# Two projections of four dropped for late batches, and VectorE's products with the sines written to the other 64 partitions

## The chip, the cores and the metric

One core of one Trainium2 chip runs the whole program. The metric is the device time of one execution in microseconds; the time before is the median of 3 runs, 332.85 us. Times of a timeline are counted from the start of the profiled execution's span.

## The reference

Two layers on x of shape (8, 256, 128): a batch b is x[b], 256 tokens of 128 features. The change touches only the first attention's q and k:

```python
def heads(W):
    return (x @ W.T).reshape(B, S, H, hd).transpose(0, 2, 1, 3)   # 16 heads of 8 features
Q = _rope(heads(Wq))
K = _rope(heads(Wk))
V = heads(Wv)
# _rope(t): t1, t2 = halves of the 8 features; [t1*cos - t2*sin, t2*cos + t1*sin]
s = (q @ k + LAMBDA * (q*q) @ (k*k)) * inv_sqrt_d, causal, softmax, times v
# once with Q, K and once with both halves rotated; outputs combined, times Wo
x = x + attention0(layernorm(x))
x = x + ffn0(layernorm(x))            # 128 -> 512 relu -> 128
x = x + attention1(layernorm(x))      # 16 heads, not causal
x = x + ffn1(layernorm(x))            # 384 wide, silu(gate) * up
```

## The kernel before

Each engine has its own program, written out by hand over *phases* and *slots*. A phase is one layer's attention of one batch (16 phases, layer 0's batches 0 to 7 first); a phase has 16 slots. In slot s of phase i TensorE computes the scores of head-slot s of phase i+1 (L901 and L902 in layer 0), whose row maxima VectorE takes (`maximum`, L734 and L736), and the shifted scores of phase i (L928, L930), whose exponential ScalarE takes (L572). In layer 0 POOL sets the future to zero in every odd slot (`cut`: L452 and then L455, "masking" in the text), and TensorE multiplies four heads of probabilities at a time by v (`pv`, L954). The maxima are transposed on TensorE twice per phase (`max_rows`, L911 and L912), copied by ScalarE (L576) and put into a row of the stack QS by DMA. Everything else (FFN, norms, output projections) is placed in slots by the tables STEP and STAGE_A. Engines take their instructions strictly in order and wait on semaphores. Slots are counted through from phase 0: slot 16 is slot 0 of phase 1; slots -16 to -1 lie ahead of phase 0.

PSUM has 8 banks. Three hold scores, two shifted scores, one the outputs; banks 6 and 7 are shared by all the other work, in an order that `bank_uses` works out: `into(name)` makes TensorE wait until the bank's last user has emptied it.

The stage of layer 0 for one batch (STAGE_A for batches 3 to 7, the late ones; batches 0 to 2 are done ahead of all phases):

- `variance` on VectorE (L667, L671), then `norm` on POOL (L413 to L423), transposes on TensorE (`norm_t0`, L851), copy to XT by ScalarE (L529);
- `project` on TensorE (L865): q by wq and, into the other half of the same bank, its *rotated twin* by wrq, whose columns are those of wq with the halves of each head exchanged; the same for k in another bank. Each of these float32 products of 128x128 by 128x256 shows as two records. Then v (L871) into bank 6;
- `product` on VectorE (L693): TQ = bank (128x512) times TAB (cosines, then sines with the sign of the rotation in them), once for q and once for k;
- `rotate` on POOL (L432): QR = left half + right half of TQ, once for q and once for k;
- `square` (L534) and a 16-bit copy (`high`, L546) on ScalarE, the remainder (`low`, L698) on VectorE, and DMAs through a scratch in HBM into the stacks QS and KS for the batch's phase.

In partition order the features are laid out so that partitions 0 to 63 hold the first halves of all heads and 64 to 127 the second halves: row j*16 + slot is feature j of the head of that slot.

## Time and profile before

| | |
|---|---|
| median of 3 runs | 332.85 us (332.72 to 333.4) |
| the profiled execution | 332.69 us, its span 330.9 us |
| TensorE matmul busy | 296.2 us (90%) |
| TensorE weight load busy | 212.9 us (64%) |
| VectorE busy | 252.3 us (76%) |
| ScalarE busy | 217.7 us (66%) |
| POOL busy | 160.7 us (49%) |
| mean granted TensorE clock | 0.973 |

A timeline row has start, duration (of several merged instructions, from the first start to the last end), engine, line, operation, tiles out<-in, shape, count, and in brackets the idle time before it and what ended it. A granted clock of 1.00 is 2.4 GHz, of 0.50 it is 1.2 GHz. The span's layer-0 stage for late batches lies between 22 and 105 us.

### The profile page before, as it was taken

To read this page: it belongs to the slowest core of one execution; us is meant where nothing else is said; L and a number is where in the kernel's file an instruction comes from. 1 tells how busy PE (TensorE), PEld (TensorE's weight loads), DVE (VectorE), ACT (ScalarE), POOL (GpSimd) and SP (SyncE) were. 2 spreads that over 40 slices of the span, in tenths; PEclk is the share of its full clock that TensorE was granted. 3 is DMA by queue.
4 is the path that set the end of the run, shared out by engine and by line. 5 is a ranking of instruction groups with operands and counts; after the bars stand their busy time and mean duration, and the time that the engine had idled before them with its cause. 6 is when DMAs were issued, how large, how long until landed. Compare 5 with 4: busy or idle time off the path is not lost.

```text
span 330.9 us, 8407 instructions
## 1 busy us (share of the span) xinstructions
PE 296.2 (90%) x2852; PEld 212.9 (64%) x2852; DVE 252.3 (76%) x999; ACT 217.7 (66%) x494; POOL 160.7 (49%) x376
## 2 busy tenths in 40 slices
PE   7648779698999899999999999999999999998945
PEld 4526556476677677767776676766767676665634
DVE  7878869688778767677768677679797979795564
ACT  8652575557568858586767768597777767677621
POOL 5641674866775867767677614523241404040210
PEclk9986799899999999999999999999999999999997
DMA  7976214311313113121211110020212010100001
GB/s 198 317 167 154 64 53 111 113 31 36 99 48 115 49 52 80 51 81 38 70 25 54 32 57 26 24 58 27 72 27 75 24 43 26 42 2 18 15 3 32
DMA packets 23178, 21.59 MB, mean 65 GB/s; under 512 B 2944, under 2 KB 20096, under 8 KB 23136
## 3 DMA queue, kind: packets, MB, share of 16 engines
q1 hardware_dynamic: 23136, 21.05, 22.9%
q8 instruction: 23, 0.38, 0.5%
q14 instruction: 19, 0.16, 0.2%
HBM read 13.18 MB, written 7.34 MB: 62 GB/s over the span
## 4 chain that ended last, share of the span: by engine, by line
PE 64%; DVE 12%; POOL 10%; issue 7%; ACT 6%; POOLq 0%; ACTq 0%; DVEq 0%
PE bank L954 15%; PE bank L928 7%; PE bank L984 5%; PE bank L997 5%; PE bank L904 4%; PE bank L905 4%; PE bank L932 4%; PE bank L1029 3%; POOL XN L423 3%; PE bank L1037 3%; PE bank L851 2%; ACT PB L572 2%; PE bank L902 2%; POOL RS L416 2%; DVE JUNK L736 2%
## 5 line engine op out<-in xcount | busy, mean ns | idle before, releaser
L572 ACT ACTIVATE PB<-bank 128x384 f32<-128x384 f32 (+1 forms) x256 | 134.6, 544 | 57.0 <-PE bank L930 34.1
L739 DVE TENSOR_REDUCE NM<-bank 128x2 f32<-128x512 f32 x128 | 83.8, 684 | 25.0 <-PE bank L905 24.8
L928 PE MATMUL bank<-QS,KS 128*128 128x256 f16 x256 | 70.5, 276 | 2.6 <-ACT PB L572 1.9
L954 PE MATMUL bank<-PB,VP 128*32 128x256 f32 (+1 forms) x1024 | 62.1, 360 | 2.5 <-POOL PB L455 1.7
L734 DVE CUSTOM_DVE_ANT_0 JUNK<-bank,MSF 128x128 bf16<-128x128 f32 x128 | 36.5, 285 | 26.1 <-PE bank L902 25.9
L736 DVE CUSTOM_DVE_ANT_0 JUNK<-bank,MSF 128x256 bf16<-128x256 f32 x128 | 53.7, 420 | 0.0
L954 PEld LDWEIGHTS bank<-PB,VP 128*32 128x32 f32 x1024 | 26.8, 109 | 25.6 <-issue 10.3
L455 POOL TENSOR_SCALAR_AFFINE_SELECT PB<-PB 128x512 f32<-128x512 f32 x64 | 41.0, 641 | 0.0
L902 PE MATMUL bank<-KS,QS 96*128 96x256 f16 x128 | 36.1, 285 | 0.0
L904 PE MATMUL bank<-KS,QS 96*128 96x256 f16 x128 | 35.2, 275 | 0.0
L905 PE MATMUL bank<-KS,QS 96*128 96x256 f16 x128 | 34.7, 271 | 0.0
L932 PE MATMUL bank<-QS,KS 128*128 128x256 f16 x128 | 34.4, 271 | 0.0
L901 PE MATMUL bank<-KS,QS 96*128 96x128 f16 x128 | 29.2, 230 | 5.7 <-DMA KS<-scr 3.5
L928 PEld LDWEIGHTS bank<-QS,KS 128*128 128x128 f16 x256 | 24.8, 97 | 12.2 <-ACT PB L572 9.6
L452 POOL TENSOR_TENSOR HELD<-EPSC 128x1 f32<-128x1 f32 x64 | 13.7, 213 | 38.1 <-ACT PB L572 38.0
L413 POOL TENSOR_TENSOR VE<-MV,EPSC 128x2 f32<-128x2 f32 x32 | 6.7, 208 | 49.0 <-DVE MV L671 49.0
L478 POOL TENSOR_TENSOR xs<-xs,Y 128x256 f32<-128x256 f32 x6 | 4.3, 725 | 49.3 <-DVE Y L748 49.3
L930 PE MATMUL bank<-QS,KS 128*128 128x128 f16 x128 | 28.1, 220 | 0.0
L423 POOL TENSOR_SCALAR XN<-xs,NMN,RS 128x128 f32<-128x128 f32 x54 | 25.4, 479 | 2.8
L416 POOL TENSOR_TENSOR RS<-VE,EPSC 128x2 f32<-128x2 f32 x32 | 22.4, 700 | 2.5
L851 PE MATMUL bank<-IDF,XN 128*128 128x128 f32 x64 | 13.5, 294 | 9.8 <-POOL XN L423 4.2
L901 PEld LDWEIGHTS bank<-KS,QS 96*128 96x128 f16 x128 | 12.8, 100 | 13.5 <-DVE NM L736 6.2
(95 smaller groups left out, 601.0 us busy)
## 6 DMA issues: line engine op xcount, KB each, us to landing
scr<-PR SPq DMA_DIRECT2D x16, 256.0 KB, 2.9
QS<-scr SPq DMA_DIRECT2D x16, 128.0 KB, 2.7
QS<-scr SPq DMA_DIRECT2D x32, 64.0 KB, 2.9
KS<-scr SPq DMA_DIRECT2D x32, 64.0 KB, 2.8
KS<-scr SPq DMA_DIRECT2D x16, 128.0 KB, 3.1
scr<-PR SPq DMA_DIRECT2D x16, 128.0 KB, 1.9
out_x<-xs SPq DMA_DIRECT2D x8, 128.0 KB, 1.9
W<-in_w SPq DMA_DIRECT2D x1, 576.0 KB, 5.9
```

The lines of the kernel that those rows point to most:

```text
L455: pool.affine_select(out=pr, in_=pr, compare_op=ALU.is_ge, fill=0.0, base=0, pattern=[[0, 4], [1, P]], channel_multiplier=-1).then_inc(s_c ...
L572: act.activation(PB[:, s % RING, 0:n], scored(i, s)[:, 0:n], ACT.Exp).then_inc(s_e, 1)
L734: dve.tensor_tensor_reduce(JUNK[:, g % 3, 0], o[:, 0:P], MSF[:, 1], -1.0, 3e38, ALU.add, ALU.min, accum_out=m[:, s, 0:1])
L736: dve.tensor_tensor_reduce(JUNK[:, g % 3, 1:3], o[:, P:3 * P].rearrange("q (n k) -> q n k", n=2), MSF[:, :], -1.0, 3e38, ALU.add, ALU.min, ...
L739: dve.tensor_reduce(m[:, s, 0:2], o[:, :].rearrange("q (n k) -> q n k", n=2), AX.X, ALU.max, negate=True).then_inc(s_mx, 1)
L901: pe.matmul(o[:, 0:P], q[:, 0:P], k[:, 0:P], start=True, stop=True)
L902: ins = pe.matmul(o[:, P:3 * P], q[:, P:2 * P], k[:, :], start=True, stop=True)
L904: pe.matmul(o[:, 0:S], q[:, 0:P], k[:, :], start=True, stop=True)
L905: ins = pe.matmul(o[:, S:2 * S], q[:, P:2 * P], k[:, :], start=True, stop=True)
L928: pe.matmul(o[:, 0:S], k[:, 0:P], q[:, :], start=True, stop=True)
L932: ins = pe.matmul(o[:, S:2 * S], k[:, P:2 * P], q[:, :], start=True, stop=True)
L954: ins = pe.matmul(o, v, pr, start=(g % 2 == 0 and kt == 0), stop=True, skip_group_check=True)
```

## The change

For batches 3 to 7 the rotated twins are not projected. `project_late` puts q (256 columns) and k (256 columns) into the two halves of one bank, bank 7, always; `product_both` replaces the two products: part 0 multiplies both by the cosines (128 partitions, 512 elements each), part 1 multiplies by the sines in two instructions over 64 partitions, each reading one half of the partitions and writing the other half. Part 0 runs in k's slot, part 1 one slot later, and only the end of part 1 frees the bank. The sines' signs now come from the half that is read, so `rotate_both` on POOL subtracts, q and k in one instruction of 128x512. It takes the place of the two rotations at the slot behind (`rot`), and the squares' slots move: sq_q by one slot (batch 3 from -4 to -3, 4 from 8 to 9, 5 from 19 to 20, 6 from 31 to 32, 7 from 47 to 48); batch 7's k rotation moves from slot 52 to slot 47. Batches 0 to 2 are as they were.

```diff
@@ -68,12 +68,12 @@
 LAST_T = (3, 4, 0, 1)
 
 
-STAGE_A = {3: dict(bn=None, norm=None, xT=-8, q=-6, k=-5, v=-3, rot_q=-4, rot_k=-3, sq_q=-4, sq_k=-2, hi=-1, lo=1),
-           4: dict(bn=-2, norm=0, xT=3, q=5, k=6, v=7, rot_q=7, rot_k=8, sq_q=8, sq_k=10, hi=12, lo=14),
-           5: dict(bn=6, norm=10, xT=13, q=15, k=17, v=18, rot_q=18, rot_k=20, sq_q=19, sq_k=21, hi=22, lo=24),
-           6: dict(bn=18, norm=22, xT=27, q=28, k=29, v=30, rot_q=30, rot_k=32, sq_q=31, sq_k=33, hi=35, lo=37),
-           7: dict(bn=34, norm=39, xT=43, q=44, k=45, v=46, rot_q=46, rot_k=52, sq_q=47, sq_k=53, hi=55, lo=57)}
-A_BANK = {3: (6, 6, 7, 6), 4: (6, 6, 7, 6), 5: (6, 7, 6, 7), 6: (6, 6, 7, 6), 7: (6, 6, 7, 6)}
+STAGE_A = {3: dict(bn=None, norm=None, xT=-8, q=-6, k=-5, v=-3, rot=-3, sq_q=-3, sq_k=-2, hi=-1, lo=1),
+           4: dict(bn=-2, norm=0, xT=3, q=5, k=6, v=7, rot=8, sq_q=9, sq_k=10, hi=12, lo=14),
+           5: dict(bn=6, norm=10, xT=13, q=15, k=17, v=18, rot=19, sq_q=20, sq_k=21, hi=22, lo=24),
+           6: dict(bn=18, norm=22, xT=27, q=28, k=29, v=30, rot=31, sq_q=32, sq_k=33, hi=35, lo=37),
+           7: dict(bn=34, norm=39, xT=43, q=44, k=45, v=46, rot=47, sq_q=48, sq_k=53, hi=55, lo=57)}
+A_BANK = {3: (6, 7, 6), 4: (6, 7, 6), 5: (6, 7, 6), 6: (6, 7, 6), 7: (6, 7, 6)}
 
 
 LOADS = {(L, b): (L * B + b - 2, "mid") for L in range(2) for b in range(B) if (L, b) > (0, 1)}
@@ -123,7 +123,7 @@
         uses += [(-100 + 4 * b + n, k, (name, b)) for n, (name, k) in
                  enumerate((("xT0", p), ("q", 2 + 3 * p), ("k", 3 + 3 * p), ("v0", 4 + 3 * p)))]
     for b, a in STAGE_A.items():
-        uses += [(a[step], k, (name, b)) for name, step, k in zip(("xT0", "q", "k", "v0"), ("xT", "q", "k", "v"), A_BANK[b])]
+        uses += [(a[step], k, (name, b)) for name, step, k in zip(("xT0", "qk0", "v0"), ("xT", "q", "v"), A_BANK[b])]
     for i in range(NPH):
         uses += [(H * (i - 1) + m0_slot(i - 1), 6 if phase(i - 3)[0] == 1 else 7, ("mr0", i)), (H * i + m1_slot(i), 6, ("mr1", i))]
         L, b = ORDER[i]
@@ -431,6 +431,12 @@
                 p = b % 2
                 pool.tensor_tensor(QR[p][:, n, 0], TQ[p][:, n, 0:S], TQ[p][:, n, S:2 * S], ALU.add).then_inc(s_rot, 1)
 
+            def rotate_both(b):
+                pool.wait_ge(*emptied("qk0", b))
+                pool.wait_ge(s_lo, 2 * b - 2)
+                p = b % 2
+                pool.tensor_tensor(QR[p][:, :, 0], TQ[p][:, :, 0:S], TQ[p][:, :, S:2 * S], ALU.subtract).then_inc(s_rot, 2)
+
             def spread_v(i):
                 L, b = ORDER[i]
                 if L == 0:
@@ -499,9 +505,8 @@
                     for b, a in STAGE_A.items():
                         if a["norm"] == H * i + s:
                             norm(0, b)
-                        for n, step in enumerate(("rot_q", "rot_k")):
-                            if a[step] == H * i + s:
-                                rotate(b, n)
+                        if a["rot"] == H * i + s:
+                            rotate_both(b)
                     if i == -1 and s == 3:
                         pool.wait_ge(s_vz, 2)
                         for p in range(2):
@@ -692,6 +697,17 @@
                 dve.wait_ge(*filled(name, b))
                 dve.tensor_tensor(TQ[p][:, n], psum(name, b)[:, :], TAB[:, n], ALU.mult).then_inc(*empties(name, b))
 
+            def product_both(b, part):
+                p, half = b % 2, P // 2
+                qk = psum("qk0", b)[:, :].rearrange("q (n t) -> q n t", n=2)
+                if part == 0:
+                    dve.wait_ge(*filled("qk0", b))
+                    dve.tensor_tensor(TQ[p][:, :, 0:S], qk, TAB[:, :, 0:S], ALU.mult)
+                    return
+                dve.tensor_tensor(TQ[p][0:half, :, S:2 * S], qk[half:P], TAB[half:P, :, S:2 * S], ALU.mult)
+                dve.tensor_tensor(TQ[p][half:P, :, S:2 * S], qk[0:half], TAB[0:half, :, S:2 * S],
+                                  ALU.mult).then_inc(*empties("qk0", b))
+
             def low(b, n):
                 p = b % 2
                 dve.wait_ge(s_hi, 2 * b + n + 1)
@@ -809,9 +825,9 @@
                             if b == 4:
                                 dve.wait_ge(s_x[3], 16)
                             variance(0, b)
-                        for n in range(2):
-                            if a["qk"[n]] == H * i + s:
-                                product(b, n)
+                        for part in range(2):
+                            if a["k"] + part == H * i + s:
+                                product_both(b, part)
                         if a["lo"] == H * i + s:
                             for n in range(2):
                                 low(b, n)
@@ -864,6 +880,16 @@
                 for half, w in enumerate(((wq, wrq), (wk, wrk))[n]):
                     ins = pe.matmul(m[:, half * S:(half + 1) * S], w, XT[0][b % 2][:, :], start=True, stop=True)
                 ins.then_inc(*fills("qk"[n], b))
+
+            def project_late(b, n):
+                if n == 0:
+                    pe.wait_ge(*emptied("xT0", b))
+                    m = into("qk0", b)
+                else:
+                    m = psum("qk0", b)
+                ins = pe.matmul(m[:, n * S:(n + 1) * S], (wq, wk)[n], XT[0][b % 2][:, :], start=True, stop=True)
+                if n == 1:
+                    ins.then_inc(*fills("qk0", b))
 
             def project_v(b):
                 m = into("v0", b)
@@ -1100,7 +1126,7 @@
                             norm_t0(b)
                         for n in range(2):
                             if a["qk"[n]] == H * i + s:
-                                project(b, n)
+                                project_late(b, n)
                         if a["v"] == H * i + s:
                             project_v(b)
 
```

## Rows read from the trace of the kernel before

**Rows 1.** Timeline of TensorE, ScalarE and VectorE, batch 3's stage, 27 to 35 us.

```profile
27.30 0.36 ACT L576 CAST MT<-bank 8x256 f16<-8x256 f32 x1 [0.42 <-PE bank L912]
...
27.38 1.91 PE L865 MATMUL bank<-XT,W 128*128 128x256 f32 x4
...
30.67 0.69 DVE L693 TENSOR_TENSOR TQ<-bank,TAB 128x512 f32<-128x512 f32 x1
...
31.28 0.28 DVE L734 CUSTOM_DVE_ANT_0 JUNK<-bank,MSF 128x128 bf16<-128x128 f32 x1
...
32.94 0.48 DVE L667 BATCH_NORM_STATS2 STAT<-xs 128x6 f32<-128x128 f32 x2
```

**Rows 2.** Timeline of TensorE, VectorE and POOL, batch 4's stage, 36 to 50 us.

```profile
38.17 2.01 PE L865 MATMUL bank<-XT,W 128*128 128x256 f32 x4
...
41.23 1.13 PE L865 MATMUL bank<-XT,W 128*128 128x256 f32 x4
...
42.40 0.69 DVE L693 TENSOR_TENSOR TQ<-bank,TAB 128x512 f32<-128x512 f32 x1 [0.94 <-PE bank L865]
...
44.44 0.27 PE L911 MATMUL bank<-IDF,NM 128*8 128x128 f32 x1 [0.58 <-DVE NM L736]
...
45.88 0.20 POOL L452 TENSOR_TENSOR HELD<-EPSC 128x1 f32<-128x1 f32 x1
...
48.79 0.44 PE L851 MATMUL bank<-IDF,XN 128*128 128x128 f32 x2 [1.49 <-POOL XN L423]
```

**Rows 3.** Timeline of TensorE, ScalarE and POOL, batch 5's stage, 50 to 64 us.

```profile
53.00 1.10 PE L865 MATMUL bank<-XT,W 128*128 128x256 f32 x4 [0.22 <-ACT MT L576]
...
57.02 0.19 POOL L452 TENSOR_TENSOR HELD<-EPSC 128x1 f32<-128x1 f32 x1 [2.15 <-ACT PB L572]
...
57.12 1.00 ACT L572 ACTIVATE PB<-bank 128x384 f32<-128x384 f32 x2
...
58.45 0.20 POOL L452 TENSOR_TENSOR HELD<-EPSC 128x1 f32<-128x1 f32 x1
...
63.59 0.80 PE L954 MATMUL bank<-PB,VP 128*32 128x256 f32 x8 [1.69 <-POOL PB L455]
```

**Rows 4.** Timeline of ScalarE, batch 6's stage, 70 to 79 us.

```profile
74.37 0.42 ACT L534 ACTIVATE QR<-QR 128x256 f32<-128x256 f32 x1
...
74.93 0.49 ACT L572 ACTIVATE PB<-bank 128x384 f32<-128x384 f32 x1
```

**Rows 5.** Timeline of VectorE and TensorE, batch 7's stage, 87 to 94 us.

```profile
88.69 0.69 DVE L693 TENSOR_TENSOR TQ<-bank,TAB 128x512 f32<-128x512 f32 x1 [0.17 <-PE bank L865]
...
90.83 0.66 DVE L693 TENSOR_TENSOR TQ<-bank,TAB 128x512 f32<-128x512 f32 x1
...
91.96 0.29 DVE L734 CUSTOM_DVE_ANT_0 JUNK<-bank,MSF 128x128 bf16<-128x128 f32 x1
...
92.74 0.27 PE L911 MATMUL bank<-IDF,NM 128*8 128x128 f32 x1 [0.19 <-DVE NM L736]
```

**Rows 6.** Groups by line and shape, whole span: count | busy us, mean ns | idle before.

```profile
L865 PE MATMUL bank<-XT,W 128*128 128x256 f32 x64 | 18.8, 428 | 1.7 <-ACT XT L529 1.4 <-ACT MT L576 0.2
...
L432 POOL TENSOR_TENSOR QR<-TQ 128x256 f32<-128x256 f32 x16 | 11.8, 738 | 9.8 <-DVE TQ L693 9.8
...
L495 POOL TENSOR_TENSOR PR<-QR,PR 128x512 f16<-128x512 f32 x8 | 9.2, 1156 | 1.6 <-ACT PR L631 1.6
...
L522 ACT COPY KS<-ZO 32x2048 f32<-32x2048 f32 x1 | 1.9, 1894 | 0.0
...
L522 ACT COPY KS<-ZO 96x2048 f32<-96x2048 f32 x1 | 1.9, 1892 | 0.0
```

**Rows 7.** Windows: length; busy (count) of PE, PEld, DVE, ACT, POOL; granted clock; DMA; GB/s.

```profile
33.22:36.64 3.42, 1.73 (x16) 1.22 (x17) 3.21 (x19) 2.51 (x6) 2.67 (x6) 1.00 0.01 1
...
36.64:40.05 3.41, 3.41 (x15) 2.36 (x15) 2.72 (x19) 1.35 (x3) 2.46 (x6) 0.50 0.50 154
...
46.90:50.30 3.40, 1.85 (x24) 1.05 (x24) 1.97 (x13) 2.90 (x8) 3.14 (x8) 1.00 0.02 4
```

## The prediction

> **What bounds the kernel now.** I read the page first. TensorE is busy 90% of the span, VectorE 76% (the table of the profile), so a change that takes work from TensorE and gives some to VectorE looks like a gain. But a share is a mean, and the change touches only the first 105 us. So I read the chain of waits there, the groups by form for durations, windows for the granted clock, and then the timeline of each engine, batch by batch. To see in them: TensorE runs through a slot's list in a fixed order and is held, again and again, by something that another engine does last. Its transposes for batch 5 wait 1.49 us for POOL's normalised x, its probs-times-v group in slot 26 waits 1.69 us for POOL's masking, its transposes of the maxima wait for VectorE [rows 1 to 5]. The projections lie between such waits. What counts is thus whether the *next* wait ends earlier.
>
> **What the change costs and removes.** TensorE [rows 6]: each projection of q or k is 4 records before, 2 after. 5 batches x 2 x 2 = 20 records go; 64 records are busy 18.8 us, 0.294 us each, so 5.9 us less work.
>
> VectorE: a product of 128x512 takes 0.69 us, and the next instruction starts 0.61 us after it (30.67 to 31.28, [rows 1]). Before there are two per batch; after there are three of 512 elements per partition, two of them over 64 partitions. No row has a product over 64 partitions. For the step from one to the next I take 0.69 rather than 0.61: the 0.08 us of overlap is shown between instructions that start in the same partitions, and the halves read from one half and write to the other. So the second part of a batch costs 2 x 0.69 = 1.38 us in one piece (bounds 0.6 and 1.5), and VectorE has 0.6 to 0.8 us more to do per batch.
>
> The Trainium skill has a rule that bears on this, in VectorE: DVE Perf Modes, section "Two Vector instructions with no wait between them": an instruction whose input or output starts in another group of 32 partitions than the last one's waits until all earlier ones have finished. No row of this trace shows it; by it both halves and the maximum behind them lose their overlap, and the sum below would be as it stands; without it some 0.35 us less.
>
> POOL: two sums of 128x256 at 738 ns become one of 128x512. The nearest row with two inputs and 512 columns is the subtraction on L495, 1156 ns, with 16-bit output [rows 6]; the upper bound is 2 x 738 = 1476. I take 1.2 us. POOL does about 0.25 us less per batch, but in one piece that can't start before the last half product, and both squares on ScalarE now wait for it. ScalarE is in order: behind the first square stand the exponentials of the next slots.
>
> Banks: q and k now share bank 7, taken when q starts and freed after the second half product, one slot later than k was. Behind it in bank 7 wait the transposed maxima (batch 4, slot 9) or the transposes xT1 (slots 31 and 47), and TensorE with them.
>
> **Batch 3 (slots -6 to -3).** q moves to bank 7, which the copy of the maxima must empty first: it runs from 27.30 to 27.66, so q starts at 27.73 rather than 27.38 [rows 1]. This is at the lower clock: its 4 records, 1.91 us with the last one's tail of 0.2 [rows 1], hold TensorE for 1.71 us, so half is 0.86. Then a slot of 0.32 and the k half, 0.86: k is there at 29.9, before at 30.67, when the product started. VectorE then has the first part (0.61), the second part (1.38) and three maxima before the statistics of batch 4; three maxima took 32.94 - 31.28 = 1.66 us. 29.9 + 0.61 + 1.38 + 1.66 = 33.55, against 32.94: **+0.6**. On these statistics hang POOL's normalisation and TensorE's transposes of batch 4. The rotation itself ends about 1.4 us later than the k rotation did and delays the first exponential by some 2 us, but the transposes come later still, so that is hidden as long as it is under about 2 us.
>
> **Batch 4.** q's 4 records start at 38.17 and end about 39.98 at the lower clock [rows 2, 7]; half is 0.9. k's at 41.23 give 0.46. With the 0.6 from batch 3, and 0.2 because more of slot 6 now falls in the slow stretch, the k half ends at 42.2 + 0.6 - 0.9 - 0.46 + 0.2 = 41.6 and the first part starts at about 41.7. From the start of the k product at 42.40 to the maxima's transposes at 44.44 [rows 2] VectorE did that product, the statistics of batch 5 and the maximum of slot 7, 2.04 us with the signal to TensorE. After, the same row of work holds from 41.7 to 43.6, and 1.38 for the second part follow: 45.0. The maxima's transposes start only then, because of bank 7, though TensorE comes there some 0.8 us sooner. The rotation runs to 46.1 or 46.2, and POOL's masking of slot 9, behind it, started at 45.88 [rows 2]: **+0.2** for POOL, and this leads to the normalisation for which TensorE waits at 48.79. So at 48.79 the 5.9 us of relief have left nothing, and 0.2 is lost.
>
> **Batch 5.** Here TensorE gains: 0.46 twice, and k no longer waits for the copy of the maxima (bank 6) at 53.00. ScalarE's exponential of slot 19 and POOL's masking of slot 19, at 57.02 [rows 3], come 1.0 us sooner, masking 55.95 to 56.7. Then POOL rotates, 56.7 to 57.9. Before, q was rotated earlier and its square was done, and the exponentials of slots 20 and 21 ran back to back from 57.12. Now the first square stands between them and waits until 57.95; the exponential of slot 21 starts 0.35 later, at 58.3, and ends at 58.8. POOL's masking of slot 21 starts at 58.85 instead of 58.45: **+0.4**. From there POOL is busy without a gap until the masking of slot 23, for which TensorE waits at 63.59 [rows 3].
>
> **Batch 6.** TensorE is 0.9 ahead, VectorE's second part ends near 71.8 and TensorE waits for bank 7 (xT1) until then. Masking of slot 31 and rotation end at 73.75; square, exponential, square on ScalarE (0.42, 0.50, 0.42 us [rows 3, 4], less about 0.1 of overlap at each: 1.05 together) bring the exponential of slot 34 to 74.85, before 74.93 [rows 4]: **0**.
>
> **Batch 7.** VectorE is without a gap through these slots but for 0.17. The product of q with its idle time goes (0.77, at 88.69), so the first part starts at 90.83 - 0.77 = 90.06; 0.61 + the maximum of slot 46, 0.55, + 1.38 = 92.6 for the maximum of slot 47, before 91.96 [rows 5]. The transposes of the maxima, 92.74, follow by **+0.6**; the FFN projection and ScalarE's relus, back to back, come after. TensorE waits for bank 7 meanwhile, with xT1 in front of it.
>
> **Sum.** 0.2 + 0.4 + 0 + 0.6 = +1.2 us, which nothing behind slot 57 gives back, since all later starts hang on each other. The profiled execution took 332.69 us (span 330.9), 0.16 under the median of 332.85; 332.69 + 1.2 = 333.9, on the median 334.05. I say **334.0**.
>
> **Rivals.**
> 1. *TensorE's relief is carried.* For: it is the busiest engine, and its projections are in the chain of waits. If the halves cost half (0.3 us), bank 7 is free before TensorE wants it; and if ScalarE doesn't stall, 0.77 (batch 4, 42.2 less the 0.6 not lost) and 0.92 for each of batches 5 to 7 come through: -3.5 us, **329.3**; where only one or two do, 331 to 332. It decides at the point where the second part ends before TensorE reaches the next user of bank 7. Against: the fills, and POOL's waits. Chance 0.15, with the partial cases.
> 2. *Nothing net.* Steps of 0.61 and a rotation of 1.16 bring batch 4 to -0.1, batch 5 to 0.3, batch 7 to 0.45: +0.65, the uncertainty of each of the four stages about 0.3: 332.3 to 333.5, say **333.0**. Chance 0.22.
> 3. *The clock falls once more.* TensorE was busy 1.73 us of the stretch from 33.22, and behind it the granted clock was 0.50; it was busy 1.85 us in that from 46.90, and the clock held [rows 7]. The change takes work out and makes the waits before it longer. If the clock falls at 50.3, 3.4 us at half speed cost up to 1.7, of which the lead of 0.9 in batch 5 may pay half: +0.8 to +1.7 on top, **335.3**. Chance 0.15. The Trainium skill, TensorE: Matmul & The Clock Gate, Part 1, says that the clock has two levels and goes by how busy TensorE has been; the trace agrees, with 0.50 and 1.00 and nothing between.
>
> **Numbers.** Forecast as summed: chance 0.48, own range 333.3 to 335.0. Below 0.2% (0.67 us; about what this measurement can tell from no change) lies 0.05 of it. Slower: 0.43 + 0.15 = 0.58. Same: 0.22 + 0.05 = 0.27. Faster: 0.15. Range: rival 3 at its upper end above, the partial cases of rival 1 below: 331.5 to 335.8.
>
> **What would show it.** 20 projection records fewer; VectorE's half products at 0.69 us each, ten of POOL's short sums (L432) gone and five of about 1.2 us in their place; TensorE waiting for VectorE before the maxima's transposes of slot 9 and the xT1 transposes of slots 31 and 47; ScalarE's squares in batches 5 and 7 waiting for POOL; the wait at 63.59 still there. Wrong, if half products take 0.35 us, if the five sums take under 1 us, if the lead of TensorE is seen past slot 26, or if the low stretches of the clock are other in number.

## The result, and the profile of the changed kernel

The changed kernel takes 336.11 us (median of 9 runs, 333.79 to 337.53), the kernel before 332.67 us in the same job. The ratio is 1.0116, 95% interval 1.0080 to 1.0153: slower by 3.9 us, and 0.3 us beyond the upper end of my range. Unless it is said to be of means or of a profile, a difference in us is the ratio less one, times the 332.5 us of the kernel before. Three runs of all, 701.97 and 335.27 us of the kernel before and 338.02 us of the one with batches 4 and 6 changed, are counted as slow and stand in no ratio and no mean. The profiled execution took 337.53 us. The head of its page, with the busy times of the span and the granted clock in 40 slices:

```profile
span 335.8 us, 8357 instructions
...
PE 296.4 (88%) x2832; PEld 212.0 (63%) x2832; DVE 256.1 (76%) x1004; ACT 217.6 (65%) x494; POOL 160.2 (48%) x371
...
PEclk9975697979999999999999999999999999999997
```

TensorE is as long busy as before (296.4 and 296.2 us) with 20 projections' records fewer; that fits the longer time at the lower clock, read below. The groups by line and shape (columns as in [rows 6]):

```profile
L890 PE MATMUL bank<-XT,W 128*128 128x256 f32 x20 | 9.3, 557 | 0.8 <-ACT XT L534 0.6 <-ACT MT L581 0.2
...
L438 POOL TENSOR_TENSOR QR<-TQ 128x512 f32<-128x512 f32 x5 | 6.4, 1270 | 10.1 <-issue 10.1
...
L707 DVE TENSOR_TENSOR TQ<-bank,TAB 64x512 f32<-64x512 f32 x5 | 3.5, 694 | 0.2
L705 DVE TENSOR_TENSOR TQ<-bank,TAB 128x512 f32<-128x512 f32 x5 | 3.4, 685 | 1.5 <-PE bank L890 1.5
L708 DVE TENSOR_TENSOR TQ<-bank,TAB 64x512 f32<-64x512 f32 x5 | 3.4, 684 | 0.1
```

A product over 64 partitions takes what one over 128 takes. Five joint sums take 1.27 us each.

Timeline of batch 3's stage, which answers to [rows 1]; line numbers are those of the changed kernel (L928 and L927 the first scores, L577 the exponential, L672 the statistics, L423 POOL's normalised x, L867 the transposes):

```profile
26.95 0.26 PE L927 MATMUL bank<-KS,QS 96*128 96x128 f16 x1
...
29.19 1.19 PE L890 MATMUL bank<-XT,W 128*128 128x256 f32 x2 [0.22 <-ACT MT L581]
...
31.60 0.69 DVE L705 TENSOR_TENSOR TQ<-bank,TAB 128x512 f32<-128x512 f32 x1 [0.21 <-PE bank L890]
...
32.87 0.69 DVE L707 TENSOR_TENSOR TQ<-bank,TAB 64x512 f32<-64x512 f32 x1
...
33.58 0.68 DVE L708 TENSOR_TENSOR TQ<-bank,TAB 64x512 f32<-64x512 f32 x1
34.29 0.29 DVE L750 CUSTOM_DVE_ANT_0 JUNK<-bank,MSF 128x128 bf16<-128x128 f32 x1
34.40 1.27 POOL L438 TENSOR_TENSOR QR<-TQ 128x512 f32<-128x512 f32 x1 [8.56 <-issue]
...
35.41 0.48 DVE L672 BATCH_NORM_STATS2 STAT<-xs 128x6 f32<-128x128 f32 x2
...
35.70 0.42 ACT L539 ACTIVATE QR<-QR 128x256 f32<-128x256 f32 x1 [6.65 <-POOL QR L438]
...
37.49 0.88 POOL L423 TENSOR_SCALAR XN<-xs,NMN,RS 128x128 f32<-128x128 f32 x2
...
37.62 0.49 ACT L577 ACTIVATE PB<-bank 128x384 f32<-128x384 f32 x1
...
39.15 0.64 PE L867 MATMUL bank<-IDF,XN 128*128 128x128 f32 x2
```

The same stretch before, as far as it isn't in [rows 1]:

```profile
25.57 0.26 PE L901 MATMUL bank<-KS,QS 96*128 96x128 f16 x1
...
33.55 0.48 ACT L572 ACTIVATE PB<-bank 128x384 f32<-128x384 f32 x1
...
35.02 1.38 POOL L423 TENSOR_SCALAR XN<-xs,NMN,RS 128x128 f32<-128x128 f32 x2
...
36.46 0.58 PE L851 MATMUL bank<-IDF,XN 128*128 128x128 f32 x2 [0.44 <-POOL XN L423]
```

The first row of each (25.57 before, 26.95 after) is TensorE's first scores of slot -8, ahead of everything that the change touches, and the two differ by 1.4 us because executions do: in a second profile of the changed kernel slot -8 starts at 25.41, in a second one of the kernel before at 26.58. So times are counted from slot -8. The statistics come 8.46 us behind it instead of 7.37, the first exponential 10.67 instead of 7.98, and the transposes of batch 4 at 12.20 instead of 10.89. Before, these transposes waited for POOL; now no wait stands at them: POOL's normalised x is done 11.42 us behind slot -8 instead of 10.83, 0.6 later, and TensorE itself gets there another 0.8 us behind it.

Batch 4, to set beside [rows 2]:

```profile
44.10 0.69 DVE L705 TENSOR_TENSOR TQ<-bank,TAB 128x512 f32<-128x512 f32 x1 [1.06 <-PE bank L890]
...
47.47 0.28 PE L937 MATMUL bank<-IDF,NM 128*8 128x128 f32 x1 [1.91 <-DVE TQ L708]
...
47.56 1.27 POOL L438 TENSOR_TENSOR QR<-TQ 128x512 f32<-128x512 f32 x1 [1.30 <-issue]
...
48.80 0.19 POOL L458 TENSOR_TENSOR HELD<-EPSC 128x1 f32<-128x1 f32 x1
...
51.70 0.44 PE L867 MATMUL bank<-IDF,XN 128*128 128x128 f32 x2 [0.95 <-POOL XN L423]
```

Batch 5, to set beside [rows 3]:

```profile
60.14 0.19 POOL L458 TENSOR_TENSOR HELD<-EPSC 128x1 f32<-128x1 f32 x1 [2.02 <-ACT PB L577]
...
60.88 1.27 POOL L438 TENSOR_TENSOR QR<-TQ 128x512 f32<-128x512 f32 x1
...
62.19 0.42 ACT L539 ACTIVATE QR<-QR 128x256 f32<-128x256 f32 x1 [1.75 <-POOL QR L438]
62.51 0.47 ACT L577 ACTIVATE PB<-bank 128x384 f32<-128x384 f32 x1
...
63.06 0.20 POOL L458 TENSOR_TENSOR HELD<-EPSC 128x1 f32<-128x1 f32 x1 [0.91 <-ACT PB L577]
...
68.22 0.86 PE L980 MATMUL bank<-PB,VP 128*32 128x256 f32 x16 [1.97 <-POOL PB L461]
```

Batches 6 (first two rows) and 7, to set beside [rows 4, 5]:

```profile
76.58 0.41 PE L867 MATMUL bank<-IDF,XN 128*128 128x128 f32 x2 [0.75 <-DVE TQ L708]
...
78.81 0.47 ACT L577 ACTIVATE PB<-bank 128x384 f32<-128x384 f32 x1
...
94.29 0.66 DVE L705 TENSOR_TENSOR TQ<-bank,TAB 128x512 f32<-128x512 f32 x1
...
96.95 0.29 DVE L750 CUSTOM_DVE_ANT_0 JUNK<-bank,MSF 128x128 bf16<-128x128 f32 x1
...
97.06 1.27 POOL L438 TENSOR_TENSOR QR<-TQ 128x512 f32<-128x512 f32 x1 [0.26 <-issue]
...
97.07 0.41 PE L867 MATMUL bank<-IDF,XN 128*128 128x128 f32 x2 [1.66 <-DVE TQ L708]
...
97.74 0.27 PE L937 MATMUL bank<-IDF,NM 128*8 128x128 f32 x1
...
98.49 0.41 ACT L539 ACTIVATE QR<-QR 128x256 f32<-128x256 f32 x1
```

The waits that I had named are there but for one: of TensorE for VectorE's last half product in slots 9, 31 and 47 (1.91, 0.75, 1.66 us), of ScalarE's square in batch 5 for POOL (1.75 us), and the wait at the probs-times-v group (1.97, before 1.69). ScalarE's square in batch 7 doesn't wait for POOL: the sum ends at 98.33, the square starts at 98.49 behind other work.

Windows of the stretches up to 110 us in which the granted clock was 0.50 (columns as in [rows 7]):

```profile
15.20:18.60 3.40, 3.19 (x11) 2.84 (x12) 2.21 (x9) 2.40 (x6) 2.39 (x6) 0.50 0.36 112
22.00:32.24 10.24, 8.68 (x38) 4.81 (x39) 8.61 (x52) 3.56 (x7) 0.80 (x6) 0.50 0.78 187
35.65:42.48 6.83, 5.63 (x30) 3.96 (x30) 5.92 (x38) 5.30 (x13) 4.81 (x12) 0.50 0.25 77
52.72:56.13 3.41, 3.41 (x28) 2.11 (x21) 2.58 (x11) 0.85 (x3) 1.34 (x3) 0.50 0.39 118
69.78:73.20 3.42, 3.37 (x16) 2.33 (x15) 2.54 (x18) 1.52 (x4) 2.00 (x6) 0.50 0.09 29
```

The five are 27.3 us together; in the profile of before there are three, 23.0 to 29.8, 36.6 to 40.0 and 63.9 to 67.4, together 13.7. The second profiles have four each: 23.9 us together in that of the changed kernel, 17.1 in that of the kernel before (16.7 to 20.1, 23.5 to 30.3, 37.2 to 40.6 and 50.8 to 54.2). Where the time went, by TensorE's first scores matmul of the slots, in us; in brackets how much of each stretch lay at the lower clock:

| slots | what lies there | before | before, second profile | changed | changed, second profile | forecast |
|---|---|---|---|---|---|---|
| start to -8 | nothing changed | 25.57 | 26.58 | 26.95 | 25.41 | 0 |
| -8 to 3 | batch 3 | 9.70 (4.2) | 9.51 (3.7) | 11.55 (8.1) | 11.55 (8.1) | +0.6 |
| 3 to 14 | batch 4 | 13.80 (3.4) | 13.69 (3.4) | 13.46 (4.0) | 13.32 (3.7) | -0.4 |
| 14 to 38 | batches 5, 6 | 30.44 (3.4) | 30.89 (3.4) | 31.88 (6.8) | 31.86 (6.8) | +0.4 |
| 38 to 49 | batch 7 | 13.45 (0) | 13.42 (0) | 14.11 (0) | 14.11 (0) | +0.6 |
| 49 to end | | 237.96 | 238.04 | 237.85 | 237.77 | 0 |

Without the first line the changed kernel is 3.5 us longer, and its two profiles agree in every stretch. Batches 4 and 7, where the time at the lower clock hardly changed, look as forecast. The excess lies in batch 3 and in batches 5 and 6, the two stretches in which the clock was low for 3 to 4 us more.

For batch 4 this hangs on where the stretch is cut. The forecast was summed at TensorE's transposes of the next batch's x. There the changed kernel is 1.3 us behind before batch 4 (12.20 us behind slot -8 for 10.89) and 1.5 behind after it (24.74 for 23.22): batch 4 adds 0.2 and takes nothing back, and over both batches it is 1.5 us in place of the 0.2 forecast (1.7 by the two second profiles).

### The profile page after: what moved, and what is told of

It is laid out like the page before. It is cut to its first block, busy times and chain, and to the rows that moved or that the text cites. A ratio compares the mean times of both kernels' runs of the same rounds, so it can differ in the third digit from the quotient of the medians.

```text
span 335.8 us, 8357 instructions
## 1 busy us (share of the span) xinstructions
PE 296.4 (88%) x2832; PEld 212.0 (63%) x2832; DVE 256.1 (76%) x1004; ACT 217.6 (65%) x494; POOL 160.2 (48%) x371
## 4 chain that ended last, share of the span: by engine, by line
PE 64%; DVE 12%; POOL 9%; ACT 6%; issue 6%; DMA 2%; SPq 1%; POOLq 0%; ACTq 0%; DVEq 0%
PE bank L980 14%; PE bank L954 7%; PE bank L1010 5%; PE bank L1023 4%; PE bank L930 4%; PE bank L931 4%; PE bank L958 4%; PE bank L1063 3%; PE bank L1055 3%; POOL XN L423 3%; ACT PB L577 2%; PE bank L928 2%; PE bank L867 2%; DVE JUNK L752 2%; PE bank L890 2%
## 5 line engine op out<-in xcount | busy, mean ns | idle before, releaser
L577 ACT ACTIVATE PB<-bank 128x384 f32<-128x384 f32 (+1 forms) x256 | 134.7, 545 | 55.4 <-PE bank L956 32.6
L461 POOL TENSOR_SCALAR_AFFINE_SELECT PB<-PB 128x512 f32<-128x512 f32 x64 | 41.7, 651 | 0.0
L928 PE MATMUL bank<-KS,QS 96*128 96x256 f16 x128 | 37.9, 299 | 0.0
L927 PE MATMUL bank<-KS,QS 96*128 96x128 f16 x128 | 30.4, 237 | 5.8 <-DVE NM L752 3.3
L930 PE MATMUL bank<-KS,QS 96*128 96x256 f16 x128 | 35.2, 275 | 0.0
L931 PE MATMUL bank<-KS,QS 96*128 96x256 f16 x128 | 34.6, 271 | 0.0
L956 PE MATMUL bank<-QS,KS 128*128 128x128 f16 x128 | 28.8, 225 | 0.0
L423 POOL TENSOR_SCALAR XN<-xs,NMN,RS 128x128 f32<-128x128 f32 x54 | 25.1, 475 | 2.8
L867 PE MATMUL bank<-IDF,XN 128*128 128x128 f32 x64 | 13.8, 300 | 12.8 <-DVE XN L683 4.4
L927 PEld LDWEIGHTS bank<-KS,QS 96*128 96x128 f16 x128 | 13.3, 104 | 14.6 <-DVE NM L752 7.0
```

The costliest lines, as they stand in the source:

```text
L461: pool.affine_select(out=pr, in_=pr, compare_op=ALU.is_ge, fill=0.0, base=0, pattern=[[0, 4], [1, P]], channel_multiplier=-1).then_inc(s_c ...
L577: act.activation(PB[:, s % RING, 0:n], scored(i, s)[:, 0:n], ACT.Exp).then_inc(s_e, 1)
L927: pe.matmul(o[:, 0:P], q[:, 0:P], k[:, 0:P], start=True, stop=True)
L928: ins = pe.matmul(o[:, P:3 * P], q[:, P:2 * P], k[:, :], start=True, stop=True)
L930: pe.matmul(o[:, 0:S], q[:, 0:P], k[:, :], start=True, stop=True)
L931: ins = pe.matmul(o[:, S:2 * S], q[:, P:2 * P], k[:, :], start=True, stop=True)
```

## The experiments

Over the runs of a kernel, the time at the lower clock is (1 - mean granted clock) x 2 x span, since the granted clock of every stretch here is 0.50 or 1.00. It is called *low time*: 20 us a run in the kernel before (19.9, mean of 116 runs of five jobs), 29.1 in the changed one. It stands beside each result.

**The changed kernel and the kernel before, again.** No edit.

> The changed kernel once more, as the base of this job's other kernels and for a second profile of it. Both theories: 1.0 to 1.3% slower than before. Waits: the stage times from slot 3 to slot 26 and from slot 37 to slot 49 are longer than before by the same 1.5 to 2 us and 0.7 us as in the first profile. Clock: the low stretches lie elsewhere, and the stage times differ with them; slots 13 to 26 take 1 to 1.5 us less if no low stretch falls between them.

Measured: 335.80 us, ratio 1.0117 (1.0074 to 1.0160), low time 29.1.

> The kernel before, once more, for a second profile of it and as this job's base. 1.00 of its own time by both theories. If the clock's low stretches belong to the order of work: about 13.6 us of them up to 105 us again, at about the same slots. If they come by the run: as many as in the profiles of the changed kernel, 20 to 24 us.

Measured: 332.46 us, ratio 0.9995 (0.9968 to 1.0023), low time 19.9. The difference is one of the kernels, and so is the low time. Where the low stretches lie and how many there are changes from one execution to the next: four here up to 105 us, 17.1 us, against three and 13.7 in the first profile.

**The twins' matmuls back, into the same columns.** The 20 records return, ahead of the real product; order, banks and products stay those of the change.

```diff
-                ins = pe.matmul(m[:, n * S:(n + 1) * S], (wq, wk)[n], XT[0][b % 2][:, :], start=True, stop=True)
+                for w in ((wrq, wrk)[n], (wq, wk)[n]):
+                    ins = pe.matmul(m[:, n * S:(n + 1) * S], w, XT[0][b % 2][:, :], start=True, stop=True)
```

> The changed kernel, but TensorE first multiplies by the twin's weights into the same columns, and then by wq or wk over it: TensorE's 20 records are back, all else is as in the changed kernel. Clock (TensorE's missing work lets the clock fall more often, about 2 us of the 3.4): fewer low stretches, time down by 1 to 2.5 us against the changed kernel. Waits (VectorE's and POOL's order cost it all): no faster, 0 to 1 us slower, as the projections are again longer.

Measured: 338.24 us, ratio 1.0201 (1.0161 to 1.0240), low time 27.5. So the relief of TensorE is there and is worth 2.8 us beside the changed kernel, with some 1.9 us of uncertainty, as in every difference of two such ratios. And most of the low time doesn't come of the missing records: with them it is still 27.5.

**Part 1 as one product.** The exchange of the halves, and with it the rotation, is left out.

```diff
-                dve.tensor_tensor(TQ[p][0:half, :, S:2 * S], qk[half:P], TAB[half:P, :, S:2 * S], ALU.mult)
-                dve.tensor_tensor(TQ[p][half:P, :, S:2 * S], qk[0:half], TAB[0:half, :, S:2 * S],
+                dve.tensor_tensor(TQ[p][:, :, S:2 * S], qk, TAB[:, :, S:2 * S],
                                   ALU.mult).then_inc(*empties("qk0", b))
```

> The changed kernel, but part 1 is one product of 128x512 instead of two of 64x512 (it leaves the exchange of the halves out, so q and k are not rotated): VectorE has the two products of before, with the changed order, banks and sum. Waits, as I summed them: 0.8 us less in each of the stages where the second part is on the path (batches 3 and 4 together 0.7, batch 7 0.75), so 1.2 to 1.8 us faster than the changed kernel. Rival (the half products matter little, the joint sum and the squares' wait or the clock do): under 0.7 us faster.

Measured: 333.19 us, ratio 1.0037 (1.0007 to 1.0068), low time 27.8. One product of 0.69 us per batch is worth 2.7 us in the whole.

**Part 1 as two whole products**, the first into a spare tile, so that no start changes partitions; the exchange is left out here too.

```diff
+                dve.tensor_tensor(SPARE[:, b % 2], qk, TAB[:, :, S:2 * S], ALU.mult)
+                dve.tensor_tensor(TQ[p][:, :, S:2 * S], qk, TAB[:, :, S:2 * S],
                                   ALU.mult).then_inc(*empties("qk0", b))
```

> The changed kernel, but part 1 is two products over all 128 partitions, the first into a spare tile (the exchange of the halves is left out, so q and k are not rotated): VectorE has three products of 512 elements per partition, as in the changed kernel, and none changes its first partition. If the length of a third product is the cost: within 0.5 us of the changed kernel. If the change of partitions is (each held start costs the overlap of 0.08 us and 0.03 to 0.05 more, three per batch, 0.3 us): 0.5 to 1 us faster than the changed kernel, 1.5 to 2 us slower than with one product for the sines.

Measured: 335.81 us, ratio 1.0110 (1.0072 to 1.0147), low time 29.5: what the changed kernel takes. By the time of the runs the price is that of a third instruction; 0.5 us for the changing partitions couldn't be told from none. The profiles do tell it where the clock is high throughout: slots 38 to 49 take 13.80 us here, 14.11 in the changed kernel, 13.42 to 13.45 before. So of batch 7's 0.7 us, 0.3 are the changing partitions and 0.4 the rest. VectorE's timeline at batch 3 in this run shows what the change of partitions itself costs:

```profile
31.18 0.68 DVE L708 TENSOR_TENSOR SPARE<-bank,TAB 128x512 f32<-128x512 f32 x1
31.79 0.68 DVE L709 TENSOR_TENSOR TQ<-bank,TAB 128x512 f32<-128x512 f32 x1
32.38 0.28 DVE L751 CUSTOM_DVE_ANT_0 JUNK<-bank,MSF 128x128 bf16<-128x128 f32 x1
```

From start to start 0.61 and 0.59 us; in the changed kernel (32.87, 33.58, 34.29) it is 0.71 twice, so 0.10 to 0.12 us for each such start, three per batch. With that the rule of the Trainium skill weighed in the prediction (VectorE: DVE Perf Modes, "Two Vector instructions with no wait between them") agrees: in the changed kernel each of these starts comes only after the 0.68 to 0.69 us of the product before it, here it comes before its end.

**The order alone.** The kernel before with its twins, banks and two products per batch, but the products in k's slot and the one behind, one joint sum (an addition), and the squares' changed slots.

```diff
-                        for n, step in enumerate(("rot_q", "rot_k")):
-                            if a[step] == H * i + s:
-                                rotate(b, n)
+                        if a["rot"] == H * i + s:
+                            rotate_both(b)
...
-                            if a["qk"[n]] == H * i + s:
+                            if a["k"] + n == H * i + s:
                                 product(b, n)
```

> The kernel before with the changed order alone: twins projected, banks as before, two products of 128x512, but the second in the slot behind k's, one joint sum on POOL (an addition), squares in the changed slots. The output is the reference's. VectorE does no more than before. If the half products are most of the cost (as the kernel with one product for the sines says, 2.6 us of 3.4): 0.5 to 1.2 us slower than before. If the order with its joint sum is as dear by itself: 1.5 us or more slower.

Measured: 336.90 us, ratio 1.0144 (1.0103 to 1.0186), low time 25.8. The new order by itself, without TensorE's saving and without a third product, costs 4.8 us, at least as much as the whole change. In batch 7 it costs nothing: slots 38 to 49 take 13.36 us.

**Which half of the order.** First the joint sum and the squares' slots without the second edit above, then the second edit without the first.

> The kernel before with only the joint sum (one addition of 128x512 per late batch) and the squares in the changed slots; products in their old slots. If the joint sum and ScalarE's wait behind it are what the changed order costs: 2.5 to 4.5 us slower than before. If it is the products' slots: under 1.5 us slower.

Measured: 335.83 us, ratio 1.0110 (1.0056 to 1.0165), low time 25.3.

> The kernel before with only the products moved: q's into k's slot, k's into the slot behind; sums of 128x256 apart, in their old slots, squares in theirs. If the later products (and the banks they free later) are what the order costs: 2 to 4 us slower than before. If it is the joint sum: under 1.5 us slower. The two together should come to the 4.4 us of both, if they don't hide behind each other.

Measured: 333.16 us, ratio 1.0032 (0.9993 to 1.0070), low time 20.9. So the joint sum with the squares behind it is worth 3.7 us of the 4.8, the later products 1.1, the latter at the edge of what the interval tells. Timeline of the joint sum alone in batch 5 (POOL's sum L439, square L540, exponential L578):

```profile
57.03 0.20 POOL L459 TENSOR_TENSOR HELD<-EPSC 128x1 f32<-128x1 f32 x1 [2.85 <-ACT PB L578]
...
57.17 0.64 POOL L462 TENSOR_SCALAR_AFFINE_SELECT PB<-PB 128x512 f32<-128x512 f32 x1
...
57.77 1.28 POOL L439 TENSOR_TENSOR QR<-TQ 128x512 f32<-128x512 f32 x1
...
59.08 0.42 ACT L540 ACTIVATE QR<-QR 128x256 f32<-128x256 f32 x1 [1.75 <-POOL QR L439]
...
59.41 0.47 ACT L578 ACTIVATE PB<-bank 128x384 f32<-128x384 f32 x1
...
59.95 0.19 POOL L459 TENSOR_TENSOR HELD<-EPSC 128x1 f32<-128x1 f32 x1 [0.91 <-ACT PB L578]
```

This kernel runs level with the one before up to slot 14 (48.94 and 49.07 us). Its masking of slot 21 starts at 59.95, before at 58.45 [rows 3]: 1.5 us later, for the exponential of that slot stands behind a square that waits 1.75 us for the sum. From the masking of slot 19 to that of slot 21 it is 1.43 us in every profile in which batch 5 has two sums in their old slots and 2.92 or 2.93 in every profile with one joint sum and the first square one slot behind its old place, whatever the clock does around it: 1.5 us for the joint sum there. Between slots 14 and 38 this run loses 3.3 us, and it has a low stretch from 64.0 to 70.8 where the profile of before has one from 63.9 to 67.4.

**The sum in two parts**, each with its own signal, in the changed kernel.

```diff
-                pool.tensor_tensor(QR[p][:, :, 0], TQ[p][:, :, 0:S], TQ[p][:, :, S:2 * S], ALU.subtract).then_inc(s_rot, 2)
+                for n in range(2):
+                    pool.tensor_tensor(QR[p][:, n, 0], TQ[p][:, n, 0:S], TQ[p][:, n, S:2 * S],
+                                       ALU.subtract).then_inc(s_rot, 1)
```

> The changed kernel, but POOL does the sum of q and then that of k, two of 128x256, with a signal each, in the same slot. ScalarE's first square then starts 0.55 us sooner after the start of POOL's sums. Waits on the joint sum (batches 5 and 7: ScalarE's exponential behind the first square): 0.5 to 1 us faster than the changed kernel. If POOL's own order sets the time: 0.1 to 0.6 us slower, as two sums take 1.46 us and the joint one 1.27.

Measured: 334.83 us, ratio 1.0105 (1.0063 to 1.0146), low time 30.1. No gain in the runs that can be told from none: both parts still start only behind the last half product. In batch 5 of its profile the first square does come sooner, as expected: masking of slot 19 to masking of slot 21 takes 2.37 us instead of 2.92.

**The banks and the squares eased.** First q and k in bank 6 for batches 3, 4, 6 and 7, so that they don't share with the maxima or xT1; then sq_q one slot later in batches 4 to 7.

```diff
-A_BANK = {3: (6, 7, 6), 4: (6, 7, 6), 5: (6, 7, 6), 6: (6, 7, 6), 7: (6, 7, 6)}
+A_BANK = {3: (6, 6, 7), 4: (6, 6, 7), 5: (6, 7, 6), 6: (6, 6, 7), 7: (6, 6, 7)}
```

> The changed kernel, but q and k of batches 3, 4, 6 and 7 share bank 6 and v takes bank 7; batch 5 is as it was, since the maxima's second transposes take bank 6 between its q and its k. TensorE's transposes of the maxima in slot 9 and xT1 in slots 31 and 47 don't wait for VectorE's part 1 any more, and batch 3's q doesn't wait for the copy of the maxima. If those waits cost time: 0.4 to 1.2 us faster than the changed kernel, most of it at slots 9 and 47. If VectorE's queue is what is late there (the maximum behind part 1 is needed just as late): within 0.4 us.

Measured: 336.24 us, ratio 1.0111 (1.0069 to 1.0154), low time 28.2. In its profile the stretches -8 to 3 and 3 to 14 are 10.99 and 12.59 us, 1.4 less than in the changed kernel, but the time of the runs doesn't show it.

> The changed kernel, but ScalarE's first square stands one slot later in batches 4 to 7 (10, 21, 33, 49), behind the exponential of that slot. If the stall of the exponentials behind the first square costs time: POOL's masking of slot 21 starts about 0.4 us sooner, and the whole is 0.5 to 1 us faster than the changed kernel. If POOL, busy with the joint sum, is as late anyway: within 0.3 us.

Measured: 334.73 us, ratio 1.0070 (1.0041 to 1.0098), low time 29.2: 1.5 us below the changed kernel, the intervals of the two overlapping. In batch 5 of its profile the maskings of slots 19 and 21 are 1.97 us apart instead of 2.92, those of slots 21 and 23 are 4.82 instead of 4.33: half of the gain is lost at once.

> The changed kernel with three of its waits eased at once: q and k in bank 6 and v in bank 7 (but batch 5), POOL's sums apart, the first square a slot later. If these waits add up: 1.5 to 2.5 us faster than the changed kernel, still 1 to 2 us slower than before. If only VectorE's extra product counts: within 1 us of the changed kernel.

That one has the three edits together. Measured: 335.95 us, ratio 1.0098 (1.0067 to 1.0128), low time 27.7. They don't add up.

**Which batches.** The change everywhere but in batch 3; then in batch 3 alone; then in batches 4 and 6 alone, with the banks eased; then everywhere but in batch 3 with all three edits. In each, the lines of STAGE_A and A_BANK of the other batches are those of the kernel before, and their q and k go through `project`, `product` and `rotate`.

> The changed kernel, but batch 3 is done as before the change (twins, two banks, two products, two sums); batches 4 to 7 are changed. All five changed-type profiles lie 1.2 to 1.9 us behind the first profile of before at slot 3, and have the clock low for 10.2 us there instead of 6.8. If batch 3 costs this: 1.0 to 1.8 us faster than the changed kernel, low time 3 to 6 us less. If it is the other batches, which lose it one by one: under 0.5 us.

Measured: 334.62 us, ratio 1.0069 (1.0036 to 1.0102), low time 22.3.

> The kernel before with the change in batch 3 alone; batches 4 to 7 as before. If batch 3 is the stage that was mis-sized: 1.2 to 2.2 us slower than before, +1.5 us or more at slot 3, and low clock of 25 to 29 us a run instead of 20. If the changed kernel's low clock comes from batches 4 to 7: under 0.7 us slower, low clock near 20 us.

Measured: 333.98 us, ratio 1.0063 (1.0030 to 1.0095), low time 27.0. In its profile the stretch -8 to 3 is 11.55 us, 8.1 of it at the lower clock, as in the changed kernel. Slots 3 to 14, unchanged work, then take 12.94 us and give 0.8 of the 1.85 back; slots 38 to 49 are back at 13.42. Batch 3 alone costs 2.1 us, the other four together 2.3, and batch 3 brings most of the low time.

> The change in batches 4 and 6 alone, where the stage times of the changed kernel show no loss (slots 3 to 10 and 27 to 37), with q and k in bank 6 and v in bank 7; batches 3, 5 and 7 as before. If the losses belong to batches 3, 5 and 7: no slower than before, or up to 1 us faster. If each batch that has the third product costs its share: 0.6 to 1.5 us slower than before.

Measured: 334.10 us, ratio 1.0035 (1.0000 to 1.0070), low time 21.3.

> The change in batches 4 to 7 with the three waits eased (q and k in bank 6 and v in bank 7 but for batch 5, sums apart, first square a slot later), batch 3 as before. If batch 3 and those waits are the whole loss: as before or up to 1 us faster. If VectorE's third product costs on its own in batch 7, where VectorE has no gap: 0.5 to 1.2 us slower than before.

Measured: 335.74 us, ratio 1.0103 (1.0069 to 1.0137), low time 26.0. It was to be better than the one without easing (1.0069) and isn't; I have no cause for that.

**Another form: no twins, but everything in the old order.** q and k keep their own banks, slots and sums; each is multiplied in three products of 256 elements. The second kernel leaves batch 3 as before.

```diff
+                if b >= 3:
+                    half, t = P // 2, psum(name, b)[:, 0:S]
+                    dve.tensor_tensor(TQ[p][:, n, 0:S], t, TAB[:, n, 0:S], ALU.mult)
+                    dve.tensor_tensor(TQ[p][0:half, n, S:2 * S], t[half:P], TAB[half:P, n, S:2 * S], ALU.mult)
+                    dve.tensor_tensor(TQ[p][half:P, n, S:2 * S], t[0:half], TAB[0:half, n, S:2 * S],
+                                      ALU.mult).then_inc(*empties(name, b))
+                    return
```

> The old order, slots, banks and sums, but no twins from batch 3 on: q and k go each into the left half of a bank of its own, and VectorE makes three products of 256 elements per partition for each of them (cosines over 128 partitions, sines twice over 64, exchanged). Output is the reference's. VectorE does 6 short products instead of 2 long ones, about 2.3 us per batch instead of 1.22, TensorE has 5.9 us less. If the order is the cost and TensorE's relief real (2.4 to 3.7 us): as fast as before or up to 2 us faster. If VectorE's time is what counts: 1 to 3 us slower than before.

Measured: 335.18 us, ratio 1.0101 (1.0068 to 1.0135), low time 28.0.

> As the kernel with three short products per tensor, but batch 3 as before, where VectorE is without a gap and TensorE isn't. If batch 3 alone costs more than it gives, as with the changed order: 0.5 to 1.5 us faster than that kernel, and the best of all.

Measured: 334.90 us, ratio 1.0052 (1.0014 to 1.0089), low time 22.2. With the joint sum gone the time is still no better; six products per batch are the likely reason, which wasn't tested apart. In both profiles slots 38 to 49, all at the higher clock, take 14.62 us, 1.2 more than before. No version here beats the kernel before.

## Why the prediction was right and wrong

**The steps that failed.** Two, and the runs name both. In batch 3 I had written off the delay of the first exponential as hidden by later transposes; it was 2.7 us and not hidden, and over batches 3 and 4 the loss was 1.5 us, not 0.2. And the sum had the clock as it was: it had no term for more time at the lower clock, which is 9 us more a run; how much of the excess that causes stays open.

**Direction and waits: right.** Half products at 0.69 us, sums at 1.27 (taken as 1.2), TensorE's waits for bank 7, the square's wait. From the first part in batch 4 to the maxima's transposes I had 3.3 us (41.7 to 45.0), the trace has 3.37 (44.10 to 47.47). Batch 7 was +0.6 and is +0.7. Batch 4 was -0.4 on its own; the -0.35 of the slots is partly luck of where they are cut, by the transposes it is +0.2. Of the signs that I named, two failed: the square of batch 7 doesn't wait, and the low stretches are other in number and length (five for three in the first profiles, four each but longer ones in the second).

**Batch 3: the path that I added up held, the one that I called hidden took over.** I had +0.6. The statistics came 1.1 us late, not 0.6: k gained 0.45 us on VectorE (4.65 us behind slot -8 instead of 5.10) and not 0.77. POOL made that up, and its normalised x was 0.6 late as forecast (11.42 for 10.83). But the joint sum ended 2.1 us later than the k rotation had (8.72 for 6.60), not 1.4, and the first exponential came 2.7 us late. I had called that hidden "as long as it is under about 2 us". It is over, and the row of the transposes shows the cover gone: they no longer wait for POOL, TensorE comes to them late, out of scores at the lower clock and behind exponentials. The stretch takes 1.85 us more; at the transposes it is 1.3. The kernel with batch 3 alone changed confirms the place, with the same 11.55 us, and its runs are 2.1 us longer than before; its profile keeps 1.0 us of the 1.85 at slot 14, so that the 2.1 aren't batch 3's stretch alone.

**Rival 3, the clock, came in addition.** I had given it 0.15 and placed it in batch 5, +0.8 to +1.7 on top, 335.3. It is there as 9 us more of low time in the mean (27.2 us at least in any run of the changed kernel, the mean before is 19.9), in batch 3's stretch and in that of batches 5 and 6. A low stretch where I had placed it, though, is in the second profile of the kernel before as well (50.8 to 54.2). And TensorE's busy time in the stretch ahead, by which I had argued, doesn't sort the cases: in the changed kernel the clock held behind 1.83 us of work (45.89 to 49.30) and fell behind 2.16 us (49.30 to 52.72):

```profile
45.89:49.30 3.41, 1.83 (x27) 1.23 (x28) 3.25 (x17) 1.04 (x4) 2.10 (x5) 1.00 0.26 81
49.30:52.72 3.42, 2.16 (x24) 1.16 (x26) 2.13 (x15) 3.42 (x10) 3.12 (x10) 1.00 0.01 4
```

How much time this is can be estimated from runs of one and the same kernel, which differ among themselves too: over 295 runs of all kernels, each taken against the mean of its own kernel in its job (those of the kernel before that served as a run of its own among them), 1 us more of low time goes with 0.31 us more of time (correlation 0.71; by kernel the slope is from -0.1 to 0.6). With that rate:

| | longer than before, means of runs (before: 332.2, all jobs) | goes with low time, 0.31 us each | rest |
|---|---|---|---|
| changed | 3.9 | 2.9 | 1.0 |
| changed, again | 3.5 | 2.9 | 0.7 |
| batch 3 alone | 2.1 | 2.2 | -0.1 |
| all but batch 3 | 2.1 | 0.8 | 1.4 |
| order alone | 4.8 | 1.9 | 2.9 |
| joint sum alone | 3.8 | 1.7 | 2.1 |
| twins back | 6.3 | 2.4 | 3.9 |
| one product of sines | 1.1 | 2.5 | -1.3 |

(A rest is uncertain by about 1.2 us, as the ratios are.) The rest of the changed kernel is 0.7 to 1.0, and I had summed +1.2 of waits at an unchanged clock. By stretch it closes too: in batch 3's, 3.9 us more of low time give 1.2, and with the 0.6 forecast 1.8, measured 1.85; in that of batches 5 and 6, 3.4 give 1.1, with the 0.4 forecast 1.5, measured 1.0 to 1.4. So the sum failed at a step that wasn't in it: that the change leaves the granted clock as it was. This account is arithmetic made after the fact. No run here holds the clock fixed for the whole program, and longer waits and low time come together (a stretch that takes longer also holds more of a low one), so that it isn't shown which part of the 2.9 the clock causes. What is shown is that most of the low time isn't due to the missing matmuls (27.5 with them), and that the order alone brings 6 of its 9 us.

In one place the profiles do hold the clock fixed. From slot 14 to POOL's masking of slot 19 some executions have no low stretch and others one of 3.4 us, starting 0.6 to 1.0 us behind slot 14:

| batch 5 | no low time | 3.4 us of it | masking of slot 19 to that of 21 |
|---|---|---|---|
| as before | 7.95 (first profile of before; 8.10 with batches 4 and 6 alone changed) | 9.57 (its second, and batch 3 alone changed) | 1.43 |
| changed | 7.29 (all but batch 3 changed) | 8.17 (both profiles of the changed kernel) | 2.92 |

So 3.4 us at the lower clock go with 1.6 us more in the old work and 0.9 in the new, 0.48 and 0.26 per us: one rate doesn't hold for every stretch. At like clock TensorE's lead is 0.7 or 1.4 us where I had 1.0, and the joint sum takes 1.5 where I had 1.4. Both terms of batch 5 were of the right kind and about the right size.

In the prediction I cited the Trainium skill, TensorE: Matmul & The Clock Gate, Part 1, for a clock of two levels that goes by how busy TensorE has been. The rows agree on the levels, 0.50 and 1.00. That it goes by how busy TensorE has been isn't settled here: the order alone, which adds waits, brings 6 us of low time, but putting 20 records of work back lowers it by only 1.6 us (29.1 to 27.5).

**"The 5.9 us of relief have left nothing": right as a sum, blind in its parts.** The runs take it apart, each step with some 1.9 us of uncertainty, so that the first can't be told from nothing and the third hardly:

| step | difference in us |
|---|---|
| products later (from the kernel before) | +1.1 |
| one joint sum, squares behind it | +3.7 |
| third product and one shared bank, with twins | +1.9 |
| twins left out | -2.8 |
| together | +3.9 |

The relief is worth 2.8 us, not nothing (3.6 with two products per batch: 1.0144 to 1.0037), and the joint sum, which I had costed as a saving of 0.25 us of POOL per batch with a wait attached, has the highest price of the four. In batch 5 I had this wait: the masking 1.0 us ahead, then 0.4 late, so 1.4 for the sum, and alone it is 1.5. I hadn't taken it for each batch by itself, nor asked what the same relief would bring without it. Where its price falls isn't the same everywhere: 1.5 us in batch 5, nothing in batch 7 (13.42 us with the joint sum alone).

**Rivals 1 and 2** are out (rival 2 was also added up wrongly, its +0.65 gives 333.5 and not 333.0): the interval begins at 1.0080, and bank 7 is free only after TensorE wants it in batches 4, 6 and 7.

**Left open:** how much of the time the low clock causes in the whole; why moving the squares helps alone and not with the rest; why bank 6 shortens two stretches of a profile and no run; and why the clock falls where it does.

## What to carry to other kernels

Merging two small operations into one saves a fixed cost per instruction (here 0.2 us per batch on POOL), but the consumer of the first half then waits for the last producer of both; look at what stands in order behind that consumer, which here was an exponential on the path. Test the order of a change apart from its saving, since both can be large and of opposite sign. Where the profile before shows stretches at half clock, put the clock into the sum as a term of its own, with a rate read from runs of one kernel, and not as a rival. Take two profiles of each kernel before reading one against the other, and compare stretches that had the same clock.

## What the runs showed of the hardware

- Single executions of one kernel on one core spread by more than 1% (330.3 to 334.5 us in 17 runs of the kernel before, with low times from 15 to 25 us), and about half of the variance goes with low time (correlation 0.71).
- 3.4 us at the lower clock, at nearly the same place in the program, went with 1.6 us more in one order of work (7.95 to 9.57) and 0.9 us more in another (7.29 to 8.17).
- VectorE's product from PSUM takes 0.66 to 0.69 us for 512 elements per partition whether 64 or 128 partitions take part, and reading one half of the partitions and writing the other costs 0.10 to 0.12 us per start.
- A POOL operation with two float32 inputs and float32 output takes 0.72 to 0.79 us for 256 elements per partition and 1.27 for 512.
